# A software loop of two batches per round, written out on every engine (audio tower, 16 batches, one core)

## What is computed

```python
h = _L0_tok_ref(x, kernel, bias)           # convolution of 9 taps, scaled by the window's norm, tanh, relu
h = h + _L0_attn_ref(_layernorm(h), ...)   # one head; three banded softmaxes (radius 12, 84, 90) averaged, Wo, layer norm
h = h + _L0_ffn_ref(_layernorm(h), ...)    # per token and each of 8 heads: scores against 2 x 64 keys, top 16 of each,
                                           # top 16 of their sums, softmax, gelu of the chosen experts' products, weighted sum
```

## Time and profile before

| what | value |
|---|---|
| median of 3 runs | 1391.68 us (1388.91 to 1394.45) |
| profiled execution | 1389.55 us |
| its span, first to last instruction | 1387.7 us |
| DVE busy | 1284.9 us, 93% |
| PE busy | 1029.8 us, 74% |
| POOL busy | 940.4 us, 68% |
| ACT busy | 919.2 us, 66% |
| mean granted clock of TensorE | 0.759 |
| first `res` (body 0) to last (body 15) | 49.2 to 1245.2 us |

### The profile page before, as it was taken

How to read it: one execution, slowest core, us unless ns; L and a number is a source line. 1 busy time by engine, 2 the same in 40 slices (tenths; PEclk the granted TensorE clock), 3 DMA queues, 4 the chain that set the end, 5 groups by cost and what they waited for, 6 DMA issues and landing times.

```text
span 1387.7 us, 41186 instructions
## 1 busy us (share of the span) xinstructions
PE 1029.8 (74%) x9585; PEld 679.4 (49%) x9585; DVE 1284.9 (93%) x10050; ACT 919.2 (66%) x4155; POOL 940.4 (68%) x1947
## 2 busy tenths in 40 slices
PE   4767777877777777778778777786778878776753
PEld 2434554645455454555446454553545545463433
DVE  4349999999999989999899998999999999999995
ACT  2576867668586857858576784767658676766532
POOL 4438776786867768577677867676776777668552
PEclk7787786769788776878877696787868778685555
DMA  2100000000000000000000000000000000000000
GB/s 55 18 15 2 3 11 3 4 8 6 10 4 11 4 5 11 4 10 4 12 4 5 9 6 10 4 12 3 5 9 5 6 3 5 4 4 5 3 4 7
DMA packets 22512, 10.97 MB, mean 8 GB/s; under 512 B 13920, under 2 KB 22032, under 8 KB 22242
## 3 DMA queue, kind: packets, MB, share of 16 engines
q1 hardware_dynamic: 21618, 7.79, 2.5%
q10 hardware_dynamic: 624, 0.30, 0.1%
HBM read 4.58 MB, written 3.01 MB: 5 GB/s over the span
## 4 chain that ended last, share of the span: by engine, by line
DVE 60%; issue 15%; PE 8%; ACT 7%; POOL 6%; SPq 1%; DVEq 1%; DMA 0%; POOLq 0%; ACTq 0%
DVE idx L1466 14%; DVE val L1464 9%; DVE cr L1536 8%; DVE scores L1469 8%; DVE oh L1479 6%; DVE best L1534 4%; DVE wl L1499 3%; ACT ns_junk L863 2%; PE banks L1055 2%; DVE bns L1389 2%; DVE masked L1419 1%; POOL cs L623 1%; PE bankM L1219 1%; PE bankQ L1142 1%; ACT act_g L840 1%
## 5 line engine op out<-in xcount | busy, mean ns | idle before, releaser
L1466 DVE FIND_INDEX8 idx<-val,scores 124x8 uint16<-124x64 f32 x1536 | 304.4, 216 | 0.0
L1464 DVE MAX8 val<-scores 124x8 f32<-124x64 f32 x1536 | 210.6, 207 | 2.4 <-ACT scores L870 1.2
L1219 PE MATMUL bankM<-wl,oh 128*128 128x16 f16 x5952 | 162.8, 172 | 46.2 <-DVE wl L1499 46.2
L1219 PEld LDWEIGHTS bankM<-wl,oh 128*128 128x128 f16 x5952 | 160.0, 101 | 59.6 <-DVE wl L1499 33.2
L597 POOL TENSOR_TENSOR qscale<-nmx,power 124x16 f32<-124x16 f32 x48 | 147.8, 3079 | 45.4 <-DVE nmx L1443 45.3
L1469 DVE MATCH_REPLACE8 scores<-val,scores 124x64 f32<-124x64 f32 x768 | 151.4, 206 | 0.0
L863 ACT ACTIVATE ns_junk<-bankQ 124x32 f32<-124x32 f32 x768 | 138.0, 255 | 12.7 <-PE bankQ L1172 12.4
L1479 DVE TENSOR_SCALAR oh<-eh 128x992 f16<-128x992 int16 x384 | 135.2, 414 | 4.5 <-ACT eh L918 4.5
L863 ACT ACTIVATION_READ_ACCUMULATOR ns_junk<-bankQ 124x1 f32 x768 | 138.3, 268 | 0.0
L1108 PE MATMUL banks<-diag,probs 124*124 124x124 f32 x672 | 107.7, 327 | 25.0 <-ACT diag L808 25.0
L1227 PE MATMUL bankM<-up_x,prod 128*124 128x128 f32 x384 | 86.5, 396 | 50.5 <-DVE prod L1508 50.5
(11 more groups left out here) (196 smaller groups left out, 3067.8 us busy)
## 6 DMA issues: line engine op xcount, KB each, us to landing
x_in<-in_x SPq DMA_DIRECT2D x16, 93.8 KB
x_in<-in_x SPq DMA_DIRECT2D x16, 62.5 KB
out<-o_sb SPq DMA_DIRECT2D x16, 62.0 KB
out<-o_sb SPq DMA_DIRECT2D x16, 61.0 KB
out<-o_sb SPq DMA_DIRECT2D x16, 60.5 KB
x_in<-in_x SPq DMA_DIRECT2D x16, 31.0 KB
oh<-more SPq DMA_DIRECT2D x6, 54.0 KB
conv_w<-in_L_tok_kernel ACTq DMA_DIRECT2D x2, 128.0 KB, 3.2
```

What stands on the lines that cost most here:

```text
L1219: last = e.matmul(coef[:, g, :, :], oh[:, k, g, :, :].rearrange("p v t -> p (v t)"), wl[:, part, k, :, TG * g:TG * (g + 1)], start=k + par ...
L1464: last = v.max(out=v_[:, hd, s, best8], in_=src[:, hd, s, :])
L1466: last = v.max_index(out=i_[:, hd, s, best8], in_max=v_[:, hd, s, best8], in_values=src[:, hd, s, :])
```

## The change

`run` calls all 20 bodies as written-out code on every engine, in the order of before; the loop over `j`, its register and its branch are gone. `Batch` then always has an integer, so every threshold of a wait and every address is a constant. No step, buffer, semaphore or order of steps is changed.

```diff
         def run(eng, start, body, end):
 
             start()
-            for b in range(BEFORE, PEELED):
-                body(Batch(b // 2, b % 2))
-            with eng.Fori(PEELED // 2, B // 2 - 1) as j:
-                body(Batch(j, 0))
-                body(Batch(j, 1))
-            for b in range(B - 2, AFTER):
+            for b in range(BEFORE, AFTER):
                 body(Batch(b // 2, b % 2))
             end()
```

## The result

The written-out kernel takes 1376.67 us (median of 6 runs, 1369.63 to 1378.36), the kernel before, measured beside it, 1393.89 us. The ratio is 0.9873 with a 95% interval of 0.9846 to 0.9900. The forecast was 1373.8 us, or 0.9871 of the median it started from.

What follows compares the result with a forecast made beforehand. VectorE (DVE), busy 93% of the span, was taken as the bound. Removing its waits, 8.6 + 7.4 + 1.9 = 17.9 us, from the 1391.7 us median gave 1373.8 us, range 1367 to 1382.

Steps and rivals of the forecast that it cites:

- DVE's back edges: DVE's loop: issue waits before `res` and `prod` at four taken edges would go, 8.6 + 7.4 = 16.0 us.
- The rule of 108 ns: Loop branches: about 108 ns each, so four edges worth 0.4 us; set aside. Rival of record cost only: chance 0.02.
- POOL's back edge: POOL's loop: idleness before `val_s` makes DVE wait for `cs`; all 1.9 us taken off, bounds 0 and 1.9.
- PE, ACT, SyncE, register arithmetic: 0: Other engines' back edges and computed wait thresholds: counted 0; upper bounds 1.2 us for `expert`, 2 us for arithmetic.
- More code: 0: All engines, 12 written bodies becoming 20: straight code is fetched ahead, cost 0; bound +1.9 us outside the span.
- What is late next: Next batch's projection: TensorE's clock at 0.50 delays ScalarE's `eh`; DVE pays about 1.8 us in such a body.
- The sum of waits: Ten loop bodies on DVE: removed waits before `res`, `prod` and `cs`, 8.6 + 7.4 + 1.9 = 17.9 us gain.
- the check by bodies: Ten loop bodies: gain 16.0 us at the straight mean, 21.8 at 79.1 us each, 18.2 with two long ones.
- The sign for the waits: Profile after, DVE: waits for `eh` or `expert` only in bodies whose projection met the clock at 0.50.
- Slower by late fetches in straight code: DVE's newly fetched code: two 1.90 us stalls in each of ten bodies, 1411.8 us; chance 0.03.
- The rival that a wait takes the place of the one removed: DVE waits for `eh` or `expert` instead: 1387.9 us, half the bodies 1378.9; chance 0.12 (gains 7 to 14), 0.05 (less).

Runs made afterwards that it cites:

- `short_loops`: Written-out kernel plus, on VectorE ahead of each of bodies 4 to 13, a five-round loop around one semaphore increment; 1391.34 us.
- `dve_loop`: Kernel before with the other four engines written out and only VectorE keeping its loop; 1394.09 us, ratio 1.0012.
- `one_round`: Kernel before with five one-round loops, no branch taken, on PE, ACT, GpSimd and VectorE, SyncE written out; 1372.19 us, repeated at 1371.26 us.
- `dve_straight`: Kernel before with VectorE alone written out, the other four engines keeping the loop; 1375.99 us, ratio 0.9881.
- the second profile: Profile from the repeated measurement of the unchanged written-out kernel, beside the one-trip loops; 1372.51 us, ratio 0.9855.

## Why the prediction was right, step by step

- **DVE's back edges, 16.0 us.** Right in place and size: the waits before `res` and `prod` vanished, DVE alone written out brings the whole gain, and keeping only DVE's loop takes it all back. That a fetch is behind it was argued then, and is shown now: an instruction packet starts some 2 us ahead of each late instruction, with the loop head moved the second stall goes, and with the branch hinted the loop loses nothing at its back edges.
- **The rule of 108 ns.** The branch's own record lasts 56 ns at the median in `short_loops`, and a near edge costs 0.19 us with its two companions; the far edge cost 3.99 us. The Trainium skill gives a compare-and-branch about 108 ns ("Advanced Engine Details and Errata", Control Flow Timing). That is between the record and the near edge here, and by it as the whole price the four far edges would have been worth 0.4 us. What decides is another rule of the Trainium skill ("Runtime: NRT & Kernel Launch", Instruction fetch mechanics): a taken branch to code that isn't held waits for a fetch of it. The traces agree with it, by the packets at 512.1 us and at the other three edges.
- **POOL's back edge, 1.9 us.** The cause was right: `cs` waits stay with POOL's loop (2.3 us) and go without it. As a gain by itself it doesn't show: `dve_loop` stands at 1.0012.
- **PE, ACT, SyncE, register arithmetic: 0.** Right, by `dve_loop` and `one_round`. The 1.2 us of `expert` that I left standing went from these ten bodies in the profile after; in others waits for it are there (`dve_straight` has 4.3 us over the span, the kernel before 2.9).
- **More code: 0.** Right: no issue wait of over 0.3 us in the steady bodies, and 1376.56 - 1374.8 = 1.8 us outside the span, as before.
- **What is late next.** The mechanism was right, its size in the sum too small for the profiled run: I allowed for two long bodies in ten at 1.8 us, the profile had four in the loop's ten and one more in body 14, the second profile three in ten. The sum of waits has no term for them at all; only the check by bodies had. Hence 12.9 us between the profiled spans where the sum had 17.9. The medians (17.2 us) lie nearer to it, and that closeness is in part luck: the kernel before was 2.2 us slower beside the new one than in the measurement that the forecast started from, and the median of the unchanged written-out kernel moved by 4.2 us between its two measurements.
- **The sign for the waits.** Nearly right. All waits for `eh` over 1 us in bodies 1 to 14 fell in bodies with 0.50, but body 5 waited 0.3 us at 0.74, and body 1 waited 1.6 us for `expert` at 1.00, as it had before.
- **Slower by late fetches in straight code.** Did not happen. Its thresholds were each one too low: 17.9 / 1.9 = 9.4, so it would have decided from 10 stalls, and been slower by 7 us from 14.

The rival that a wait takes the place of the one removed is what the profiled pair shows: 5.8 us of `eh` came, four of the ten bodies were long, and the spans differ by 12.9 us, where this rival with half of the bodies long had 12.8. By the medians, and by the second profile with three long bodies, it is nearer to the forecast. Its reason, that DVE's stalls had given TensorE and ScalarE time to catch up, isn't shown: `dve_loop` keeps these stalls and still waits 7.9 us for `eh`.

## What to carry to other kernels

A long loop (here some 1250 DVE instructions a round) can pay a few microseconds at each taken back edge on the engine that sets the end, whatever its branch record says; a loop of a few instructions paid 0.19 us. Look for "issue" idleness at the first instructions of a round, for an instruction packet about 2 us ahead of it, and compare with a peeled body of the same trace. Writing the loop out, or only hinting its closing branch, brought the same here; writing it out on the engines with slack brought nothing. Where two chains are balanced to about a microsecond, expect part of what is taken from one to be lost to lateness of the other, here when TensorE's clock was at 0.50.

## What the runs showed that I had not expected

- The back edge pays twice, 2.09 us and then 1.90 us a few instructions later, with a packet of 8 KB before each. Moved to the start of a block the loop head pays once, which fits a head that lay shortly before the end of a fetched stretch; its place itself stands in no trace.
- With the hint the loop still fetches the code of each round (19 packets on q14) and loses nothing at its back edges. The packets of the whole span fall from 188 to 159, and 1.2 us of stall turn up behind the loop's exit.
- Forty near edges, 9.1 us of idleness, lengthened the kernel by 14.7 us; 3.2 us more of `eh` wait and 1.9 us of three smaller waits make up nearly all of the difference. Why nine of ten bodies waited for `eh` there stays open.
- The same program differs by some 4 us between profiles (spans 1374.8 and 1370.5 us) with six and four bodies that meet the clock at 0.50 in one 3.5 us stretch. What sets the phase of that clock against the bodies I didn't find out.
